# A transformer block on one Trainium2 core: the opening laid out anew, with identity products and later loads, and key spreads, residual additions and stores moved

## The reference

```python
def ffn(x):                        # W1, W3: 2048 x 512; W2: 512 x 2048
    hidden = silu(x @ W1.T) * (x @ W3.T)
    return fwht(hidden) @ W2.T     # Walsh-Hadamard transform over 2048, orthonormal

def attention(x):                  # 16 heads of 32, chunks of 128 rows
    q, k, v = split(rmsnorm(x, qkv_norm_w) @ ternary(qkv_w).T)
    for each chunk:                # state S is 32 x 32 for each head
        o = 32 ** -0.5 * (((q @ k.T) * mask) @ v + lam_t * (q @ S))
        S = lam_T * S + (lam_rev * k).T @ v
    return rmsnorm(rmsnorm(o, norm_w), proj_norm_w) @ ternary(proj_w).T

x = x + 0.5 * ffn(layernorm(x))
x = x + attention(layernorm(x))
x = x + 0.5 * ffn(layernorm(x))
```

## Time and profile before

| | us |
|---|---|
| median of 3 runs | 2373.56 |
| lowest and highest | 2372.96, 2374.03 |
| the profiled execution, own time | 2375.16 |
| its span on the core | 2373.4 |
| TensorE busy in the span | 2332.8 |
| VectorE busy | 1229.2 |
| ScalarE busy | 717.2 |

### The profile page before, as it was taken

One profiled execution on the slowest core, in us unless ns is written; L12 is line 12 of the kernel. 1 busy time (PEld: TensorE's weight loads), 2 busy tenths in 40 slices (PEclk: granted clock), 3 DMA queues, 4 the chain that ended last, 5 costly groups with the idle time before them and its releaser, 6 DMA issues.

```text
span 2373.4 us, 30927 instructions
## 1 busy us (share of the span) xinstructions
PE 2332.8 (98%) x12339; PEld 1109.7 (47%) x12339; DVE 1229.2 (52%) x2209; ACT 717.2 (30%) x1228; POOL 143.8 (6%) x102
## 2 busy tenths in 40 slices
PE   6999999999999999999999999999999999999999
PEld 3344445444444454444544454445444544544444
DVE  6586645654565445545554365544564455445312
ACT  6645323223232322233223332233233223322211
POOL 0090000000000000000000000000000000000000
PEclk9999999999999999999999999999999999999999
DMA  7947531251224322333042132421332224131200
GB/s 199 223 145 195 138 107 45 58 128 53 65 52 115 70 49 63 93 76 89 28 129 58 54 81 85 102 45 36 111 76 72 63 54 98 27 89 36 58 32 18
DMA packets 299455, 196.80 MB, mean 83 GB/s; under 512 B 231600, under 2 KB 256176, under 8 KB 295472
## 3 DMA queue, kind: packets, MB, share of 16 engines
q1 hardware_dynamic: 299024, 194.31, 31.7%
q10 hardware_dynamic: 288, 0.52, 0.1%
HBM read 84.68 MB, written 54.53 MB: 59 GB/s over the span
## 4 chain that ended last, share of the span: by engine, by line
PE 87%; DVE 3%; issue 3%; POOL 2%; DMA 2%; ACT 1%; SPq 1%; DVEq 0%; ACTq 0%; POOLq 0%
PE d_bank L1413 25%; PE l_bank L1393 25%; PE g_bank L1393 24%; PE a_bank L1448 5%; PE a_bank L1431 2%; PE a_bank L1508 2%; PE a_bank L1459 1%; POOL work L714 1%; PE a_bank L1490 1%; PE a_bank L1495 1%; POOL work L713 1%; DVE work L1122 1%; PE a_bank L1473 1%; DMA w1t<-q_parts 1%; DMA zt<-cent 0%
## 5 line engine op out<-in xcount | busy, mean ns | idle before, releaser
L1413 PE MATMUL d_bank<-w2t,work 128*128 128x512 f16 x2940 | 672.0, 379 | 1.7 <-DVE work L1122 1.7
L1413 PEld LDWEIGHTS d_bank<-w2t,work 128*128 128x128 f16 x2940 | 284.6, 98 | 334.3 <-issue 2.1
L1102 DVE SCALAR_TENSOR_TENSOR work<-l_bank,l_scale,work 128x512 f32<-128x512 f32 x256 | 191.8, 749 | 432.1 <-PE l_bank L1393 432.1
L1393 PE MATMUL g_bank<-xt,w1t 128*128 128x512 f16 x1536 | 355.0, 381 | 5.0 <-DMA w1t<-q_parts 3.1
L1393 PE MATMUL l_bank<-xt,w3t 128*128 128x512 f16 x1536 | 352.5, 379 | 2.0 <-DVE work L1102 1.7
L831 ACT ACTIVATE work<-g_bank,g_scale 128x512 f32<-128x512 f32 x256 | 175.4, 685 | 450.6 <-PE g_bank L1393 442.7
L1393 PE MATMUL l_bank<-work,w3t 128*128 128x512 f16 x1344 | 308.3, 379 | 0.2 <-DVE work L1102 0.2
L1393 PE MATMUL g_bank<-work,w1t 128*128 128x512 f16 x1344 | 308.3, 379 | 0.0
L850 ACT CAST work<-work 128x512 f16<-128x512 f32 x232 | 143.3, 618 | 525.8 <-DVE work L1102 524.3
L1393 PEld LDWEIGHTS g_bank<-xt,w1t 128*128 128x128 f16 x1536 | 147.9, 98 | 181.1 <-DMA w1t<-q_parts 5.4
L1393 PEld LDWEIGHTS l_bank<-xt,w3t 128*128 128x128 f16 x1536 | 147.7, 98 | 176.5 <-issue 2.3
(11 more groups left out here) (219 smaller groups left out, 1785.0 us busy)
## 6 DMA issues: line engine op xcount, KB each, us to landing
work<-parts_dram SPq DMA_DIRECT2D x192, 128.0 KB, 2.8
x_dram<-work SPq DMA_DIRECT2D x16, 1024.0 KB, 4.4
work<-x_dram SPq DMA_DIRECT2D x11, 1024.0 KB, 6.6
...
```

What stands on the lines that cost most here:

```text
L1102: nc.vector.scalar_tensor_tensor(out=hfull, in0=l_bank[:], scalar=l_scale[:, j:j + 1], in1=gate, op0=ALU.mult, op1=ALU.mult).then_inc(hful ...
L1393: ins = nc.tensor.matmul(dst[:], wt[:, wp, k, P * j:P * (j + 1)], src[:, xp, k, :], start=(k == 0 and wp == xp), stop=(k == KT - 1 and wp ...
L1413: ins = nc.tensor.matmul(d_bank[t][:], parts[:, hp, P * t:P * (t + 1)], w2t[:, j, wp, :], start=(j == 0 and hp == wp), stop=(j == HT - 1 a ...
```

## The change

- **Identity products.** A new step warm multiplies the 128 x 128 identity by itself into d_bank0, which nobody reads before it is written anew: 22 times at the start, 4 times after the second turn, 8 times after the fourth.
- **Opening order.** The statistics of x (new step rows) come first on DVE, ahead of the first wscale; wsum 0 and 1 come first on ACT, behind a Silu of one column. In first_steps each wprep stands one step earlier.
- **Loads.** Batch 1's x is loaded behind wprep 5 instead of at the start, and its statistics are taken in four separate steps. All of W2 is loaded behind wprep 31.
- **n = 1.** Each butterfly stage is four POOL instructions of half the size instead of two. What is needed only later of the step wfit becomes wrest, at slot 29. The ternary weights' source (4 MB) is loaded at w2pair 0.
- **w2pair** goes round four pairs of banks instead of two. Pair i from 4 on waits for pair i - 4 to be read.
- **qprep** 12 to 15 move from the end of n = 0's down to the start of n = 1's.
- **Residuals.** resid 2 and 3 move from behind low 0 to behind gate 1 of the next feed-forward, and the stores that follow resid 3 move with them. Those of n = 3 and n = 4 move on to slots 103 and 150.
- **Key spreads.** The three DMAs that spread k stand one slot later than those of q, in a step kspread. One normalisation and one reload (unpark) are moved by 6 and 5 slots.

The core of the diff (lines "@@" name the function):

```diff
-        pair_bank = [a_bank, [g_bank, l_bank]]
+        pair_bank = [d_bank[0:2], d_bank[2:4], a_bank, [g_bank, l_bank]]
@@ feed_forward
-                steps += [("gate", j)] + slots.get(base + 3 * j, []) + [("lin", j)] + slots.get(base + 3 * j + 1, [])
+                steps += [("gate", j)]
+                if j == 1:
+                    steps += [("begin", n - 1)] + finish[2:] + [("begin", n)]
+                steps += slots.get(base + 3 * j, []) + [("lin", j)] + slots.get(base + 3 * j + 1, [])
...
-                    steps += [("begin", n - 1)] + finish + [("begin", n)]
+                    steps += [("begin", n - 1)] + finish[:2] + [("begin", n)]
@@ attention_slots
                     add(slots, at - 4, [("klow", (b, g))])
+                    add(slots, at - 3, [("kspread", (b, g))])
...
+            for at, n in LATE_STORES.items():
+                add(slots, at, [("store", n)])
-            for at, b in ((19, 3), (109, 4), (253, 5), (343, 6), (461, 7)):
+            for at, b in ((19, 3), (109, 4), (253, 5), (349, 6), (461, 7)):
...
+        LATE_STORES = {103: 3, 150: 4}
@@ first_steps
-            steps = [("begin", 0), ("wsum", 0), ("wscale", 0), ("stat", key), ("wprep", 0), ("wprep", 1)]
-            steps += [("prep", (key, t)) for t in range(3)] + [("wsum", 1), ("turn", (key, 0)), ("prep", (key, 3))]
-            steps += [("turn", (key, t)) for t in range(1, TT)] + [("wscale", 1), ("wprep", 2), ("wprep", 3)]
-            steps += [("wsum", 2), ("wsum", 3), ("wscale", 2)]
+            steps = [("begin", 0), ("warm", 22), ("wsum", 0), ("wsum", 1)] + [("rows", (key, t)) for t in range(TT)]
+            steps += [("stat", key), ("wscale", 0), ("prep", (key, 0)), ("prep", (key, 1)), ("wprep", 0), ("prep", (key, 2))]
+            steps += [("turn", (key, 0)), ("prep", (key, 3)), ("turn", (key, 1)), ("wprep", 1), ("warm", 4)]
+            steps += [("turn", (key, t)) for t in range(2, TT)] + [("warm", 8), ("wsum", 2), ("wscale", 1), ("wprep", 2), ("wprep", 3)]
+            steps += [("wsum", 3), ("wscale", 2), ("wprep", 4)]
...
+            for t in range(TT):
+                add(own, 7 + 2 * t, [("rows", (("ffn1", 1), t))])
             for i, part in enumerate(norm_steps(("ffn1", 1))):
-                add(own, 10 + 2 * i, part)
+                add(own, 14 + 2 * i, part)
             for j in range(HT):
                 steps += [("gate", j)]
                 if j < HT - 2:
-                    steps += [("wprep", 2 * j + 4)]
+                    steps += [("wprep", 2 * j + 5)]
...
-                if j < HT - 2:
-                    steps += [("wprep", 2 * j + 5)]
                 if j < HT - 4 and j % 2:
                     steps += [("wscale", (j + 5) // 2)]
+                if j < HT - 3:
+                    steps += [("wprep", 2 * j + 6)]
...
-            for at, step in ((9, "wtop"), (10, "top_turn"), (11, "top_max"), (12, "top_spread"), (13, "wfit")):
+            for at, step in ((9, "wtop"), (10, "top_turn"), (11, "top_max"), (12, "top_spread"), (13, "wfit"), (29, "wrest")):
...
-                add(own, 7 + i, [("qprep", 2 * i), ("qprep", 2 * i + 1)])
+                if i < 6:
+                    add(own, 7 + i, [("qprep", 2 * i), ("qprep", 2 * i + 1)])
...
                 if j < 2:
-                    steps += [("reload", 7 + j)]
+                    steps += [("qprep", 12 + 2 * j), ("qprep", 13 + 2 * j), ("reload", 7 + j)]
...
-            return steps + [("resid", t) for t in range(TT)]
+            return steps + [("resid", t) for t in range(2)]
@@ sync
-            sp.dma_start(x_next, x[1].rearrange("(t p) d -> p t d", p=P)).then_inc(x_next_loaded, 16)
...
-                    if m and c >= 13:
-                        for t in ((0,), (1,), (2, 3))[c - 13]:
+                    if arg == 5:
+                        sp.dma_start(x_next, x[1].rearrange("(t p) d -> p t d", p=P)).then_inc(x_next_loaded, 16)
+                    if arg == 2 * HT - 1:
+                        for t in range(KT):
                             load_w2(t, 0)
                             load_w2(t, 1)
...
-                elif step == "resid" and arg == TT - 1:
+                elif step == "store" or (step == "resid" and arg == TT - 1 and n not in LATE_STORES.values()):
...
                                      parts_dram[ag % 2, 0, :, part].rearrange("(h p) t -> p h t", h=HG)).then_inc(q_moved, 16)
+                elif step == "kspread":
+                    ag = arg[0] * GROUPS + arg[1]
                     sp.wait_ge(k_stored, 16 * (ag + 1))
@@ gpsimd, butterflies
-                    nc.gpsimd.tensor_tensor(b[:, :, 0, :], a[:, :, 0, :], a[:, :, 1, :], ALU.add)
-                    ins = nc.gpsimd.tensor_tensor(b[:, :, 1, :], a[:, :, 0, :], a[:, :, 1, :], ALU.subtract)
+                    n_a = HT // 4 >> st
+                    for c in (slice(0, n_a), slice(n_a, 2 * n_a)):
+                        nc.gpsimd.tensor_tensor(b[:, c, 0, :], a[:, c, 0, :], a[:, c, 1, :], ALU.add)
+                        ins = nc.gpsimd.tensor_tensor(b[:, c, 1, :], a[:, c, 0, :], a[:, c, 1, :], ALU.subtract)
@@ scalar
+            nc.scalar.activation(tiny[:, 15:16], ident[:, 0:1], ACT.Silu)
             act.wait_ge(dve_const, 1)
@@ tensor
+                elif step == "warm":
+                    for _ in range(arg):
+                        nc.tensor.matmul(d_bank[0][:, 0:P], ident[:], ident[:], start=True, stop=True)
...
-                    else:
-                        pe.wait_ge(w2_final_lo, 2 * (i - 1))
+                    elif i >= 4:
+                        pe.wait_ge(w2_final_lo, 2 * (i - 3))
...
-                        pe.wait_ge(w2_final_lo, 2 * j + 1 if j < HT // 2 else HT)
+                        pe.wait_ge(w2_final_lo, max(2 * j + 1, 12) if j < HT // 2 else HT)
```

59 lines of the change are left out of this document (35 added, 24 removed).

## The result

The changed kernel takes 2361.71 us (median of 5 runs, 2359.46 to 2364.33) against 2373.56. The ratio is 0.9947, with a 95% interval from 0.9936 to 0.9958: 12 us faster. The forecast was 2350.0 with a range up to 2358, so it named the right side and twice the size, and the time lies outside its range. The profiled execution, 2359.46 us, is the fastest of the five.

The account below looks back on a forecast made before the run. TensorE, busy 2332.8 of 2373.4 us, was taken as the bound. Gains 5.5 + 6.3 + 3.4 + 2.0 + 1.7 + 0.9 + 1.2 + 2.6 = 23.6 off 2375.16 give 2351.6, less 1.6 for the median: 2350.0, range 2345.5 to 2358.

Parts of the forecast that it names:

- The opening: Start to gate 1: statistics first and gate 0 at 2.4 GHz bring gate 1 from 29.11 to 23.65, gain 5.5 us.
- Rival (a): Opening: identity products do not bring gate 0 to 2.4 GHz; gate 1 at 25.4, about 2351.7 us; chance 0.13.
- I leave 0.8: n = 0 from gate 1 on: of 7.1 us lost, 0.8 stay, gain 6.3 us, at worst 4.
- I leave 2.7: n = 1: of 6.1 us lost, 2.7 stay, of which 1.0 to 1.6 is the last transposed load ahead of w2pair.
- rival (d): n = 1: POOL's 24 added halves cost 0.3 us each, its chain ends 7 us later, no gain: 2353.5 us; chance 0.1.
- The gain of 3.4: n = 1: smaller POOL pieces and the moved wrest gain 3.4 us, between 2 and 4.2.
- w2pair: 64 matmuls in 13.8 instead of 15.83 us, as four pairs of banks remove waits: gain 2.0 us.
- the turn to down: Start of n = 1's down: TensorE's wait for the residual behind four pairs of qprep goes, gain 1.7 us.
- n = 4 and 5: Waits on parts_dram (1.2) and zt (1.4), behind a megabyte stored or loaded, go by LATE_STORES: gain 2.6 us.
- Residuals: From n = 2 on: splitting the four-instruction block gains 0.9 us on scores and 1.2 on three diag row waits.
- Nothing else changes in 2100 us: From n = 2 on: beyond the residual, diag row, parts_dram and zt waits, no stage changes; TensorE hardly waits there.
- Rival (c): Key spreads a slot later lose 1.0 us in each of 32 head groups: slower, about 2382 us; chance 0.05.

Follow-up runs that it names:

- the other pair: Changed kernel with batch 6's normalisation at slot 343 and batch 1's x loaded at the start: 2355.05 us with the 22 early identity products, 2353.05 us without.
- the kernel with the four together: Changed kernel with each feed-forward's four residual additions in one place again, behind low 0 of the next: 2362.51 us (one execution).
- The kernel with three edits: Changed kernel with batch 6's normalisation at slot 343, batch 1's x loaded at the start and no early 22 identity products: 2353.05 us, ratio 0.9908.

## Why the prediction was wrong, step by step

**The opening** was right: 6.4 us where 5.5 was said, by the steps named (statistics at 5.91, gate 0 at 2.4 GHz, the pieces from ACT as the bound). Two parts came otherwise. The idle time behind the 22 was 1.6 us and not 4, and the turns ran at 2.4 GHz, which the prediction had left out; in the traces where they did not, gate 0 came 0.6 to 1.5 us later. And gate 1 waited for the transposed weights of wprep 2, not for Silu 0. Rival (a) did not come.

**Gate 1 to n = 1.** The step that failed is "I leave 0.8". What was to go went: no wait is left at 100 us. But the change puts a megabyte ahead of a transposing load at 33 us, the same pattern as in the earlier trace rows, and the prediction read that pattern only as removed. What was left was 1.6 us in the profiled execution and 1.8 to 6.4 in nine others, of which waits of 0.3 to 0.7 us at 81 to 89 us are a part; with the load back at the start it was nothing. The prediction had also said that no transposed load of W1 or W3 would take over 4 us, and this one took 7.0.

**n = 1.** The step that failed is "I leave 2.7". 6.6 us are lost, 3.9 more. The largest part is shown: the 22 products cost 2.0 us here (89.5 against 87.5 without them; 90.9 against 88.7 in the other pair), by a last wait of 3.2 instead of 1.7 us and the half clock behind it, and the instruction packet among the last loads is the likely means. It stood in no term of the sum. The halves were taken as a gain and were none that can be seen: they cost 6.3 us of POOL, as rival (d) said with 7, and whole pieces give the same n = 1 within what traces differ by. A third effect, the ternary weights' quarters behind 4 MB of W2, makes a wait of 1.4 or 1.9 us in two later traces but none in this one. The gain of 3.4 became a loss of 0.5. Which further wait makes up the remaining 1.9 us is open; every placing of the splits kept at least 4.5 us of loss.

**w2pair, the turn to down, n = 4 and 5** were right to 0.6 us, though in the last the mechanism was mostly the place behind gate 1 and not LATE_STORES.

**Residuals.** Of 2.1 us, 0.6 came, and the kernel with the four together shows that none of it is due to the split; what it is due to stays open. The term took the wait behind a block as its price and did not ask what the moved half would stand ahead of.

**n = 9.** But for a diag wait of 0.4, not in the sum at all. The diff moves one number from 343 to 349, and the step that failed is "Nothing else changes in 2100 us". This was the largest miss with a single cause: 4.0 us, and up to 5.6.

**From the execution to the median.** The forecast took 1.6 off the profiled execution's time. The changed kernel's profiled execution was its fastest, 2.25 below its median, and its new waits (at 33, 184 and 1398 us) differ from trace to trace or sometimes take the clock with them; that these make the spread of the unprofiled executions too is inferred from the smaller spread without them. The kernel with three edits, without two of these waits and with the third halved, has 1.2 us of spread (and with the 22 back 2.1).

Rival (c) had no part in it: n = 4 got shorter, and no head group waits on key spreads.
